# Two causal attentions of a decoder: later keys zeroed by a select on GpSimd after the exponential, in place of a mask product on TensorE before it

## The chip, the cores and the metric

The kernel runs on one core of one Trainium2 chip. The metric is the device time of one execution in microseconds (us), the median of several runs. Each engine works through its own queue of instructions in order and waits on semaphores that other engines raise: TensorE (PE in the profile, with its weight loads as PEld), VectorE (DVE), ScalarE (ACT), GpSimd (POOL) and SyncE (SP, which here issues DMAs).

## The reference, cut to what matters

The program is a decoder of twelve sub-layers on x of 16 x 256 tokens x 128. Several of them hold attentions with a softmax; the change touches two that are causal, both with 16 heads of width 8. One is the self-attention inside `L0_xattn`:

```python
att = jnp.einsum('bhqd,bhkd->bhqk', q, k) * scale
causal = jnp.tril(jnp.ones((T, T), bool))
att = jnp.where(causal[None, None], att, -jnp.inf)
y = jnp.einsum('bhqk,bhkd->bhqd', jax.nn.softmax(att, axis=-1), v)
...
y = y + jnp.einsum('bhqk,bhkd->bhqd', jax.nn.softmax(attc, axis=-1), vc)
```

The other is `_mha` inside `L2_ffn`, with rotary q and k:

```python
causal = jnp.tril(jnp.ones((s, s), dtype=bool))
scores = jnp.where(causal, scores, -jnp.inf)
attn = jax.nn.softmax(scores, axis=-1)
y = jnp.einsum('bhqk,bhkd->bhqd', attn, v)
```

## The kernel before, in words

Each attention is an object of class `SelfAttention`; `program` makes those two with mode "causal": s1 (the first attention below; it also carries the cross-attention, `cross=True`) and s8 (the second; `rope=True`). Work goes by **units**, one batch element each, 16 per attention, and by **slots**: every engine has a method `*_slot(e, g)` that is called with g = 0, 1, 2, ... and issues what this engine has to do in slot g. The order on each queue is thus fixed by those methods; nothing reorders it. A unit starts every 10 slots in s1 and every 8 in s8. In its slots 0 to 7 the maxima pass runs, one pair of heads (s and 8 + s) per slot; in its slots 12 to 19 (LE = 12) the exponentials pass runs on the same pairs. Since these overlap with the next unit's maxima, a usual slot holds both.

**Maxima pass.** `pe_max` (L1235) multiplies q by k for two heads into PSUM banks that three rotating tiles share, `pe_max_mask` (L1253) adds a large negative mask of later keys by a product of an identity (bf16) with a 128x128 mask for both diagonal blocks (256 columns), and `dve_max` (L1269) takes row maxima. At the unit's end L1278 joins two of them, `dve_neg_max` (L615, L617) negates and splits them, `pe_mbt` (L626) turns them, ScalarE copies them (L635), and SP writes them as extra rows of q, so that the second product of q and k comes out with the maximum already subtracted.

**Exponentials pass.** `pe_exp` (L1362) writes the scores with keys on the partitions and queries along the row, two heads in two of three banks: 256 columns for the first key block and 128 for the second, 384 in all; columns 0 to 127 and 256 to 383 are the diagonal blocks. `pe_exp_mask` (L1378) adds the mask to these two blocks by one product of 256 columns per head, and signals `st`. `act_exp` (L1322) takes the exponential into PT, which holds four pairs. Two slots later, in slots with odd s, `pe_pv` (L1417) multiplies two pairs of PT by the values, 16 products; the 9th column of the values is one and gives the sum of the exponentials. `act_tv`, `pe_tvt` (L659), `dve_norm` (L670, L676) and `pe_oot` (L699) finish a unit.

**Everything else in the slots.** Every two units `Tail` does the output product (L281), the residual (L295) and the norm. Its inverse root is seeded on VectorE by L418, L420, L422 and refined on GpSimd by `newton`, three rounds of the four lines L429, L431, L433, L435, each of which waits for the one before. In s8 the norm also takes L351, L352 on GpSimd and L365, L367, L377 on VectorE. q and k are split into three bf16 parts (ScalarE L571, L577; GpSimd `pool_rest` L582 and `pool_lo` L588) and stacked by DMA; in s8 VectorE L1089 and GpSimd L1096 (`pool_rope`) rotate them first. In s1 GpSimd also adds the cross part (L1462).

Of the kernel before, what the change touches and what calls it, by code (L numbers as in the profile page):

```python
# [8 lines left out]
ALU = mybir.AluOpType  # L9
# [891 lines left out]
def twice(mask):  # L901
    return mask.rearrange("p (o k) -> p o k", o=1).to_broadcast([128, 2, 128])


class SelfAttention(Heads):


    LE, MBT, CMBT, TV, GATE = 12, 9, 11, (5, 9, 11), 8

    def __init__(self, K, prev, W, mode, rope=False, reps=1, gate=False, cross=False, kind="ln", g=None, lead=0, ring=0, again=False):  # L910
# [8 lines left out]
        LE, L = self.LE, 10 if cross else 8  # L919
# [3 lines left out]
        start = [P + s for s, _, _ in rows]  # L923
# [14 lines left out]
        nu = len(units)  # L938
# [29 lines left out]
        self.st = K.ev("scores", 2 * nu * self.nx)  # L968
        self.exp = K.ev("exp", nu * self.nx if mode == "bias" else 2 * nu * self.nx)
        self.biased = K.ev("scores_biased", nu * self.nx if mode == "bias" else 0)  # L970
        self.pv = K.ev("pv", nu * self.np)
        self.tv = K.ev("tv", nu * self.nf)
        self.tvt = K.ev("tv_turned", nu * self.nf)
# [373 lines left out]
    def pe_exp(self, e, u, s):  # L1347
        K, mode = self.K, self.mode
        b, r = self.units[u]
        c, bb = b // 2, b % 2  # L1350
        x = self.nx * u + s
        plain = mode == "none"
        if s == 0:
            e.wait_ge(*self.shift.at(u))
        self.banks_free(e, x)
        lo = 128 if self.causal else 0
        rows = self.mrow + 2
        for kt in range(2):
            for i in self.heads(x):
                q1 = K.QS[self.set(c)][64 * i:64 * i + rows, s, 256 * bb + lo * kt:256 * bb + 256]  # L1360
                k1 = K.KS[self.set(c)][64 * i:64 * i + rows, s, 256 * bb + 128 * kt:256 * bb + 128 * kt + 128]
                k = e.matmul(self.st_bank(x, i)[:, 256 * kt:512 - lo if kt else 256], k1, q1, start=kt == 0,  # L1362
                             stop=plain and kt == 1)
                if plain and kt == 1:
                    k.then_inc(*self.st.inc())

    def pe_exp_mask(self, e, u, s):
        K, mode = self.K, self.mode
        if mode == "none":
            return  # L1370
        x = self.nx * u + s
        for i in self.heads(x):
            hh = 8 * i + s
            s_ = self.st_bank(x, i)
            if mode == "bias":
                k = e.matmul(s_[:, 256:384], K.idf[:, :], self.bias.KB[:, hh, 0:128], start=False, stop=True)
            elif mode == "causal":
                k = e.matmul(s_.rearrange("p (a k) -> p a k", a=2)[:, :, 0:128], K.idb[:, :], twice(K.mskK[:, :]), start=False,  # L1378
                             stop=True)
            elif mode == "add":  # L1380
                diag = s_.rearrange("p (a k) -> p a k", a=4)[:, 0:4:3, :]
                k = e.matmul(diag, K.idb[:, :], twice(self.mask[:, 256:384]), start=False, stop=True)  # L1382
            k.then_inc(*self.st.inc())

    def dve_bias(self, e, u, s):

        K = self.K
        x = self.nx * u + s
        lo = self.BANKS[x % 2][0]
        st = K.PS[:, lo:lo + 2, 0:256]  # L1390
        e.wait_ge(*self.scored(x))
        e.tensor_tensor(st, st, self.bias.KB[:, s:16:8, :], ALU.add).then_inc(*self.biased.inc())  # L1392

    def pt_free(self, x):

        if x < 4:
            return None
        u, s = divmod(x - 4, self.nx)
        return self.pv.at(self.np * u + (s // 2 if s < 8 else s - 4))

    def pe_pv(self, e, u, j):
        K = self.K
        c, bb = self.units[u][0] // 2, self.units[u][0] % 2
        f = self.nf * u + j // 2
        x = self.nx * u + 2 * j
        if j % 2 == 0 and f > 0:
            e.wait_ge(*self.tv.at(f - 1))
        if j == 0 and bb == 0 and self.units[u][1] == 0:
            e.wait_ge(*(self.vact if self.W["vb"] is None else self.vdve).at(c))
        e.wait_ge(*self.exp_done(x + 1))  # L1410
        g = j % 2
        for kt in range(2):
            for i in range(4):
                lo = 128 if kt == 1 and self.causal else 0
                o = 256 if kt == 1 else 0
                pt = K.PT[:, (x + i // 2) % 4, 0:2 * self.width].rearrange("p (a k) -> p a k", a=2)
                k = e.matmul(K.PS[32 * i:32 * i + 9, 6, 256 * g + lo:256 * g + 256],  # L1417
                             K.VA[self.set(c)][:, (2 * bb + kt) * 16 + 8 * (i % 2) + 2 * j + i // 2, :], pt[:, i % 2, o:o + 256 - lo],
                             start=kt == 0, stop=kt == 1)
        k.then_inc(*self.pv.inc())  # L1420
# [271 lines left out]

    def pool_slot(self, e, g):
        K, LE = self.K, self.LE
        u = self.at(g, self.OOS - 1)
        if u is not None and (self.gate or self.cross):
            self.pool_join(e, u)
        c = self.out_at.get(g + 3)
        if c is not None and self.W["ob"] is not None:
            self.tail.pool_bias(e, c)  # L1700
        for off in (1, 4, 6):
            c = self.out_at.get(g - off)
            if c is not None:
                self.tail.pool(e, c, off)
        if self.rope:
            for n, kind, key in self.splits_at.get(g + 1, []):
                self.pool_rope(e, n)
        for n, kind, key in self.splits_at.get(g - 1, []):
            if kind != "setup":
                self.pool_lo(e, n, self.source(n, kind, key))  # L1710
        for n, kind, key in self.splits_at.get(g, []):
            if kind != "setup":
                self.pool_rest(e, n, self.source(n, kind, key))
# [198 lines left out]
class CrossAttention(Heads):  # L1912
# [5 lines left out]
    LE, turns = 5, 5  # L1918
# [2640 lines left out]
```

## Time and profile before

| what | value |
|---|---|
| median of 3 runs | 4510.38 us (4504.48 to 4520.68) |
| the profiled execution, its own time | 4514.29 us |
| its span in the profile | 4512.5 us |
| mean granted TensorE clock | 0.855 of full speed |
| busy, share of span | PE 77%, DVE 62%, ACT 46%, POOL 26% |

How to read it: all times inside the profile are of one execution, counted from the start of its span. A busy share is an average over stages whose limits differ. Matmuls are pipelined and the ends of their rows are modelled, so their starts, and those of the weight loads, tell more than their lengths. "Idle before" at the end of a row is how long this engine had been idle, and "<-" what ended it; "issue" means that nothing the profile shows was waited for. Rows with xN merge N neighbours.

### The profile page before, as it was taken

To read this page: it belongs to the slowest core of one execution; us is meant where nothing else is said; L and a number is where in the kernel's file an instruction comes from. 1 tells how busy PE (TensorE), PEld (TensorE's weight loads), DVE (VectorE), ACT (ScalarE), POOL (GpSimd) and SP (SyncE) were. 2 spreads that over 40 slices of the span, in tenths; PEclk is the share of its full clock that TensorE was granted. 3 is DMA by queue.
4 is the path that set the end of the run, shared out by engine and by line. 5 is a ranking of instruction groups with operands and counts; after the bars stand their busy time and mean duration, and the time that the engine had idled before them with its cause. 6 is when DMAs were issued, how large, how long until landed. Compare 5 with 4: busy or idle time off the path is not lost. (4 is left out here: it accounts for less than half of the span.)

```text
span 4512.5 us, 86659 instructions
## 1 busy us (share of the span) xinstructions
PE 3476.0 (77%) x30682; PEld 2227.5 (49%) x30682; DVE 2808.6 (62%) x7618; ACT 2086.9 (46%) x4656; POOL 1181.7 (26%) x2276
## 2 busy tenths in 40 slices
PE   5877888886887668738989989756994558858992
PEld 1443554453555447713444444333552445648992
DVE  4884675365786665625777767457774376865563
ACT  2664665223343535414666666443562034425661
POOL 2322221021111234520111110124321242133565
PEclk9987998797998769957999999767996579979996
DMA  4323321023220322212121110132332050022332
GB/s 96 52 34 56 56 54 22 17 90 49 34 34 16 62 65 75 75 33 34 33 34 32 30 31 17 23 63 41 56 46 67 15 155 19 5 84 77 108 95 67
DMA packets 316471, 231.39 MB, mean 51 GB/s; under 512 B 45267, under 2 KB 300848, under 8 KB 315868
## 3 DMA queue, kind: packets, MB, share of 16 engines
q1 hardware_dynamic: 303116, 199.36, 22.1%
q0 software_dynamic: 12928, 26.50, 1.9%
q8 instruction: 248, 4.06, 0.4%
q14 instruction: 179, 1.47, 0.1%
HBM read 68.43 MB, written 55.53 MB: 27 GB/s over the span
## 5 line engine op out<-in xcount | busy, mean ns | idle before, releaser
L1322 ACT ACTIVATE PT<-ps 128x512 f32<-128x512 f32 (+1 forms) x1600 | 812.0, 559 | 519.7 <-PE ps L1382 274.4
L1272 DVE TENSOR_REDUCE M<-ps 128x2 f32<-128x512 f32 x1024 | 655.6, 684 | 289.4 <-PE ps L1256 262.0
L1235 PE MATMUL ps<-SKB 49*128 49x256 bf16 (+2 forms) x3584 | 434.2, 280 | 170.9 <-DMA SKB<-HH 74.0
L1269 DVE TENSOR_REDUCE M<-ps 128x3 f32<-128x384 f32 x768 | 390.5, 550 | 187.2 <-PE ps L1253 122.0
L1417 PE MATMUL ps<-PT,VA 128*9 128x256 f32 (+1 forms) x7168 | 451.4, 371 | 1.5 <-ACT PT L1322 1.0
L1362 PE MATMUL ps<-SKB 51*128 51x256 bf16 (+2 forms) x3584 | 366.1, 271 | 88.5 <-DMA SKB<-MT 70.5
L3675 ACT ACTIVATE SKB<-ps,SKB 128x128 f32<-128x128 f32 x1032 | 295.2, 370 | 254.8 <-PE ps L3595 253.5
L1235 PEld LDWEIGHTS ps<-SKB 48*128 48x128 bf16 (+1 forms) x3584 | 138.4, 95 | 475.2 <-issue 157.5
L3737 DVE COPY SKB<-SKB 128x1028 f32 (+1 forms) x258 | 187.3, 726 | 235.1 <-PE ps L3604 206.8
L582 POOL TENSOR_TENSOR FF<-FF,HH 128x512 f32<-128x512 f32 (+1 forms) x118 | 128.8, 1092 | 605.2 <-ACT HH L571 605.0
L3595 PE MATMUL ps<-SKB 128*128 128x128 f32 x2064 | 286.3, 284 | 0.0
L3604 PE MATMUL ps<-SKB 128*128 128x128 f32 x2064 | 282.2, 281 | 3.6 <-ACT SKB L3675 3.6
L3595 PEld LDWEIGHTS ps<-SKB 128*128 128x128 f32 x2064 | 263.0, 199 | 0.4 <-issue 0.3
L3604 PEld LDWEIGHTS ps<-SKB 128*128 128x128 f32 x2064 | 260.4, 198 | 4.5 <-ACT SKB L3675 4.5
L3512 POOL DMA_INDIRECT L_sorted_rows<-XT,GG x192 | 196.9, 1026 | 246.2 <-DVE SKB L3744 120.2
L1417 PEld LDWEIGHTS ps<-PT,VA 128*9 128x9 f32 x7168 | 155.2, 91 | 199.8 <-issue 95.2
L1362 PEld LDWEIGHTS ps<-SKB 50*128 50x128 bf16 (+1 forms) x3584 | 176.7, 98 | 149.8 <-DMA SKB<-MT 81.4
L429 POOL TENSOR_TENSOR NW<-NW 128x4 f32<-128x4 f32 x336 | 69.4, 206 | 656.6 <-DVE NW L422 628.5
L3570 POOL DMA_INDIRECT PT<-L_sorted_results,GG x192 | 196.4, 1023 | 131.0 <-issue 50.7
L659 PE MATMUL ps<-idf,TV 128*128 128x128 f32 x1088 | 177.8, 288 | 33.1 <-ACT TV L650 16.2
L1313 ACT ACTIVATE PT<-ps 128x768 f32<-128x768 f32 x128 | 103.8, 811 | 212.3 <-DVE ps L1392 212.3
L1052 PE MATMUL ps<-XT,WB 128*128 128x512 f32 x224 | 152.7, 769 | 49.4 <-DMA SKB<-in_c_one 29.2
(487 smaller groups left out, 6760.2 us busy)
## 6 DMA issues: line engine op xcount, KB each, us to landing
SKB<-HH SPq DMA_DIRECT2D x1224, 64.0 KB
SKB<-HH SPq DMA_DIRECT2D x576, 32.0 KB
PT<-L_sorted_rows SPq DMA_DIRECT2D x258, 64.0 KB
L_sorted_results<-SKB SPq DMA_DIRECT2D x258, 64.0 KB
SKB<-in_L3f_w SPq DMA_DIRECT2D x32, 256.0 KB, 3.3
L_sorted_rows<-TV SPq DMA_DIRECT2D x2, 4032.0 KB, 29.0
SKB<-scratch SPq DMA_DIRECT2D x2, 2048.0 KB, 10.6
SKB<-in_L1f_w SPq DMA_DIRECT2D x16, 256.0 KB, 3.2
```

Of the source, the lines that this page charges most:

```text
L1235: k = e.matmul(self.mx_bank(m + i)[:, o:o + n], K.QS[self.set(c)][64 * i:64 * i + rows, s, 256 * bb + 128 * qt:256 * bb + 128 * qt + 128], ...
L1269: k = e.tensor_reduce(K.M3[n % 2][:, hh, 0:3], mx[:, 0:384].rearrange("p (a k) -> p a k", a=3), axis=AX.X, op=ALU.max)
L1272: k = e.tensor_reduce(K.M3[n % 2][:, hh, 0:2], mx.rearrange("p (a k) -> p a k", a=2), axis=AX.X, op=ALU.max)
L1322: e.activation(K.PT[:, x % 4, n * i:n * i + n], self.st_bank(x, i)[:, 0:n], ACT.Exp, bias=0.0, scale=self.scale).then_inc(*self.exp.inc())
L1362: k = e.matmul(self.st_bank(x, i)[:, 256 * kt:512 - lo if kt else 256], k1, q1, start=kt == 0, stop=plain and kt == 1)
L1417: k = e.matmul(K.PS[32 * i:32 * i + 9, 6, 256 * g + lo:256 * g + 256], K.VA[self.set(c)][:, (2 * bb + kt) * 16 + 8 * (i % 2) + 2 * j + i / ...
L3512: e.indirect_dma_start(self.XS[h], bass.IndirectOffsetOnAxis(ap=D.IDX[:, col:col + 1], axis=0), K.XT[:, 128 * t:128 * t + 128], None).then ...
L3570: e.indirect_dma_start(self.YG[i % 8], None, self.YS[h], bass.IndirectOffsetOnAxis(ap=D.IDX[:, q:q + 1], axis=0)).then_inc(*self.gathered. ...
L3595: k = e.matmul(K.PS[:, 2 + m % 2, 128 * hc:128 * hc + 128], self.WT[m % 3][:, 128 * hc:128 * hc + 128], self.XC[m % 3], start=True, stop=True)
L3604: k = e.matmul(K.PS[:, 4 + m % 2, 0:128], self.HB[m % 3][:, hc, :], self.WT[m % 3][:, 512 + 128 * hc:640 + 128 * hc], start=hc == 0, stop= ...
L3675: k = e.activation(self.HB[n % 3][:, hc, :], K.PS[:, 2 + n % 2, 128 * hc:128 * hc + 128], self.func, bias=self.WT[n % 3][:, 1024 + hc:1025 ...
L3737: e.tensor_copy(self.WT[n % 3], self.table[:, bass.ds(at, TC)]).then_inc(*self.wt.inc())
```

## The change

In mode "causal", `pe_exp_mask` does nothing and `pe_exp` signals `st` itself. A new `pool_select` stands at the head of GpSimd's slot LE + 1 + s: it waits for the pair's second exponential and runs two `affine_select` instructions in place on PT, one per head, on both diagonal blocks (128 x 2 x 128 elements, f32); where query minus key is negative they write 0. The second signals `selected` (it uses the counter named scores_biased), and `pe_pv` waits for it instead of for the exponential. The mask of the maxima pass stays. The four-deep PT and all other orders stay. The exponential is now also taken of later keys' scores, and the result overwritten.

```diff
@@ SelfAttention.__init__
+        self.selects = mode == "causal"
+        self.selected = K.ev("scores_biased", 8 * nu * self.selects)
@@ pe_exp
-        plain = mode == "none"
+        plain = mode == "none" or self.selects
@@ pe_exp_mask
-        if mode == "none":
+        if mode == "none" or self.selects:
             return
...
-            elif mode == "causal":
-                k = e.matmul(s_.rearrange("p (a k) -> p a k", a=2)[:, :, 0:128], K.idb[:, :], twice(K.mskK[:, :]), start=False,
-                             stop=True)
+    def pool_select(self, e, u, s):
+
+        x = self.nx * u + s
+        e.wait_ge(*self.exp_done(x))
+        for i in range(2):
+            diag = self.K.PT[:, x % 4, 384 * i:384 * i + 384].rearrange("p (b k) -> p b k", b=3)[:, 0:3:2, :]
+            k = e.affine_select(diag, diag, [[0, 2], [1, 128]], ALU.is_ge, 0.0, base=0, channel_multiplier=-1)
+        k.then_inc(*self.selected.inc())
@@ pe_pv
-        e.wait_ge(*self.exp_done(x + 1))
+        e.wait_ge(*(self.selected.at(8 * u + 2 * j + 1) if self.selects else self.exp_done(x + 1)))
@@ pool_slot
+        hit = self.inside(g, LE + 1, 8)
+        if hit and self.selects:
+            self.pool_select(e, *hit)
```

TensorE's queue in s8, a slot that ends in the value products. Before (PT holds exponentials, ps is PSUM, SKB the stacked q and k):

```order
L1235 MATMUL ps<-SKB 128x128 [waits mx_free] x2
L1235 MATMUL ps<-SKB 128x256 x2
L1362 MATMUL ps<-SKB 128x256 [waits exp]
L1362 MATMUL ps<-SKB 128x256
L1362 MATMUL ps<-SKB 128x128 x2
L1253 MATMUL ps<-mskQ,idb 128x2x128 x2
L1378 MATMUL ps<-mskK,idb 128x2x128 x2
L1417 MATMUL ps<-PT,VA 9x256 [waits exp]
```

The same slot in the changed kernel (its lines stand 3 to 9 further down):

```order
L1238 MATMUL ps<-SKB 128x128 [waits mx_free] x2
L1238 MATMUL ps<-SKB 128x256 x2
L1365 MATMUL ps<-SKB 128x256 [waits exp]
L1365 MATMUL ps<-SKB 128x256
L1365 MATMUL ps<-SKB 128x128 x2
L1256 MATMUL ps<-mskQ,idb 128x2x128 x2
L1426 MATMUL ps<-PT,VA 9x256 [waits scores_biased,tv]
```

The two products of L1378 are gone, and the value products wait for a select.

GpSimd's queue in s8 around the Newton steps of a tail (NW, RSD: the root; FF, HH: a split). Before:

```order
L351 TENSOR_TENSOR X<-X,RR 128x512
L352 TENSOR_TENSOR RR<-RR 128x512
L1096 TENSOR_TENSOR FF<-FF,GG 128x512
L582 TENSOR_TENSOR FF<-FF,HH 128x512
L429 TENSOR_TENSOR NW<-NW 128x4
...
L435 TENSOR_TENSOR RSD<-NW 128x4
L588 TENSOR_TENSOR HH<-FF,HH 128x512
L1096 TENSOR_TENSOR FF<-FF,GG 128x512
```

And in the changed kernel, from the end of the selects of one stretch to the next:

```order
L351 TENSOR_TENSOR X<-X,RR 128x512
L352 TENSOR_TENSOR RR<-RR 128x512
L1099 TENSOR_TENSOR FF<-FF,GG 128x512
L1400 AFFINE_SELECT PT<-PT 128x2x128 x2
L582 TENSOR_TENSOR FF<-FF,HH 128x512
L1400 AFFINE_SELECT PT<-PT 128x2x128 x2
L429 TENSOR_TENSOR NW<-NW 128x4
...
L435 TENSOR_TENSOR RSD<-NW 128x4
L588 TENSOR_TENSOR HH<-FF,HH 128x512
L1400 AFFINE_SELECT PT<-PT 128x2x128 x12
```

One pair's selects (x2) now stand on either side of L582, and those of six further pairs (x12) behind L588; four tails of s8 look like this, in the last ones the split (L582, L588) is absent.

## Rows read from the trace of the kernel before

**Rows 1.** The page: busy time by engine, and the chain that ended last.

```profile
PE 3476.0 (77%) x30682; PEld 2227.5 (49%) x30682; DVE 2808.6 (62%) x7618; ACT 2086.9 (46%) x4656; POOL 1181.7 (26%) x2276
...
PE 5%; POOL 1%; issue 1%; DVE 1%; DMA 0%; DVEq 0%; ACT 0%; POOLq 0%
```

**Rows 2.** Windows over s1 and s8: length, busy per engine, PEclk, DMA share, GB/s.

```profile
423.00:752.00 329.00, 297.76 (x3378) 169.48 (x3374) 228.15 (x698) 206.56 (x463) 78.63 (x151) 0.95 0.26 50
3163.00:3413.00 250.00, 235.77 (x2815) 133.12 (x2814) 185.21 (x491) 156.62 (x350) 71.80 (x131) 1.00 0.30 48
```

**Rows 3.** The mask product, L1378: count, min/median/max ns; who waited for it.

```profile
L1378 PE MATMUL ps<-mskK,idb x512: 272/273/421, 423.5 to 3412.8; 128*128 128x256 bf16 x171
...
  ACT PT L1322: 154.6, 191
```

**Rows 4.** Waits: total us, times, longest; first in s8, then in s1.

```profile
PEld ps L1235 <- DVE M L1269: 23.7, 56, 1.5
...
PEld ps L1235 <- DVE M L1269: 18.5, 46, 0.8
```

**Rows 5.** Timeline, TensorE's weight loads, s8, two slots: start, us, engine, line.

```profile
3344.48 0.11 PEld L1253 LDWEIGHTS ps<-mskQ,idb 128*128 128x128 bf16 x2 [0.16 <-issue]
3344.61 0.21 PEld L1378 LDWEIGHTS ps<-mskK,idb 128*128 128x128 bf16 x2
3345.02 0.09 PEld L1235 LDWEIGHTS ps<-SKB 48*128 48x128 bf16 x1 [0.21 <-issue]
3345.41 0.11 PEld L1235 LDWEIGHTS ps<-SKB 48*128 48x128 bf16 x3 [0.30 <-DVE M L1269]
...
3346.39 0.55 PEld L1417 LDWEIGHTS ps<-PT,VA 128*9 128x9 f32 x16 [0.21 <-issue]
3347.16 0.11 PEld L1235 LDWEIGHTS ps<-SKB 48*128 48x128 bf16 x4 [0.22 <-issue]
```

**Rows 6.** Timeline, weight loads, s8 before its first exponentials (no L1378 yet).

```profile
3153.48 0.11 PEld L1253 LDWEIGHTS ps<-mskQ,idb 128*128 128x128 bf16 x2 [0.16 <-issue]
3153.81 0.09 PEld L1235 LDWEIGHTS ps<-SKB 48*128 48x128 bf16 x1 [0.21 <-DVE M L1269]
```

**Rows 7.** Groups of instructions on GpSimd, whole run: busy us, mean ns, idle before.

```profile
L582 POOL TENSOR_TENSOR FF<-FF,HH 128x256 f32<-128x256 f32 x16 | 10.8, 675 | 50.1 <-ACT HH L571 50.1
...
L4285 POOL MEMSET SKB<- 128x2048 f32 x1 | 1.8, 1805 | 0.0
...
L3517 POOL MEMSET TV<- 128x128 f32 x2 | 0.4, 205 | 6.3 <-ACT XT L393 6.3
```

**Rows 8.** Timeline, GpSimd, s8, around one root.

```profile
3313.55 1.28 POOL L1096 TENSOR_TENSOR FF<-FF,GG 128x512 f32<-128x512 f32 x1 [5.43 <-DVE GG L1089]
3315.75 1.16 POOL L582 TENSOR_TENSOR FF<-FF,HH 128x512 f32<-128x512 f32 x1 [0.92 <-ACT HH L571]
3317.01 0.20 POOL L429 TENSOR_TENSOR NW<-NW 128x4 f32<-128x4 f32 x1
...
3320.10 0.20 POOL L435 TENSOR_TENSOR RSD<-NW 128x4 f32<-128x4 f32 x1
3320.25 1.16 POOL L588 TENSOR_TENSOR HH<-FF,HH 128x512 bf16<-128x512 f32 x1
```

**Rows 9.** Timeline, the same stretch: two exponentials, and the value products' weight loads.

```profile
3311.74 0.87 ACT L1322 ACTIVATE PT<-ps 128x384 f32<-128x384 f32 x2 [1.93 <-PE ps L1378]
3313.65 0.87 ACT L1322 ACTIVATE PT<-ps 128x384 f32<-128x384 f32 x2 [1.04 <-PE ps L1378]
...
3318.42 0.55 PEld L1417 LDWEIGHTS ps<-PT,VA 128*9 128x9 f32 x16 [0.21 <-issue]
...
3321.91 0.55 PEld L1417 LDWEIGHTS ps<-PT,VA 128*9 128x9 f32 x16 [0.21 <-issue]
```

**Rows 10.** Timeline, the same stretch: a small VectorE operation and TensorE's wait behind it.

```profile
3315.77 1.16 DVE L422 TENSOR_SCALAR NW<-NW 128x4 int32<-128x4 int32 x1
...
3317.44 0.11 PEld L1235 LDWEIGHTS ps<-SKB 48*128 48x128 bf16 x3 [1.49 <-DVE M L1269]
```

## The prediction, made before the changed kernel ran

> **What bounds the kernel now.** I read the page first. TensorE is the busiest engine, and the chain that ended last covers only 8% of the span, the experts at the very end [rows 1]; it says nothing of the two causal attentions. So I went to the windows over them [rows 2]. TensorE is busy 298 of 329 us (91%) in s1 and 236 of 250 (94%) in s8, at a granted clock of 0.95 and 1.00; VectorE stands at 69% and 74%, ScalarE at 63%, GpSimd at 24% and 29%. A slot of s8 lasts 250 / 128 = 1.95 us, one of s1 some 2.2 (16 units of 10).
>
> The waits say where TensorE is not the limit: in 56 slots of s8 and 46 of s1 its next maxima product waits for VectorE's reduce to free a bank [rows 4]. The two slots of the timeline show both kinds [rows 5]. In the first, weight loads go L1378, one L1235, and then stop 0.30 us until a reduce is done: whatever is taken from TensorE there, it waits longer. In the second, the value products follow, and the next L1235 waits for issue alone. ScalarE waits for the mask product 191 times, 154.6 us [rows 3], but it has that time to spare.
>
> **What goes.** 2 x 8 x 16 x 2 = 512 mask products [rows 3], two in each of 256 slots. The rows price the two by difference: from L1253's load to the next L1235's first load is 0.33 us where no L1378 stands between [rows 6]. With it, the same stretch is 3345.02 - 3344.48 = 0.54 us [rows 5]. So a slot gives back 0.21 us, where TensorE is what the slot waits for. In s8 that is 128 - 56 = 72 slots. In s1 128 - 46 = 82, less some 17 (my count on the timeline) at the units' ends that wait for the cross-attention's maxima: 65. 137 x 0.21 = **29 us gained**. In the other slots I cost the removal at nothing: VectorE's reduce covers it, and its chain is not touched. The exponential also starts earlier, but its bank comes free in time already, so this gains nothing.
>
> **What comes.** 512 selects on GpSimd, two per slot. No row shows one. From below: a write-only fill takes 205 ns for 128 columns and 1805 for 2048, 0.83 ns a column, so 0.31 us for 256 [rows 7]. From above: a sum of two tensors, 256 columns, takes 0.675 us [rows 7]; and this form has two blocks with a gap, which might add to that. A select reads one tensor, so I take a little under the middle: 0.45 us, **0.9 us a pair**, with 0.31 and 0.7 as ends.
> The Trainium skill (GPSIMD Engine Reference, 3.1) puts its best loop without branches at 1.8 cycles an element, 769 ns for 512; an estimate from that for 256 elements is 0.38 us plus dispatch, 0.5 to 0.6. By it a pair is about 1.1 us, and the sum below would end near 4511 us instead of 4504. No row here decides between the two.
>
> Load on GpSimd: 29% of 1.95 us is 0.57 us a slot, with a pair 1.5 us. It fits, on average. What counts is the queue. A select stands behind whatever GpSimd has in its slot, and the value products of slots with odd s need the pair of two slots before. From the end of the exponential at 3313.65 + 0.87 to the products at 3318.42 that is 3.9 us [rows 9], elsewhere down to some 2.5. It does not do where a norm's root stands in the queue. I walk through it in s8 [rows 8, 9]:
> - L1096 ends at 3313.55 + 1.28 = 3314.83. The exponentials that begin at 3311.74 are long done, so their select runs from there to 3315.75.
> - L582 follows at its old time, to 3316.9. The pair of 3313.65 is selected by 3317.85; value products at 3318.42 need it, in time.
> - The root, 3.29 us from L429's start to RSD's end, now begins at 3317.9 and ends at 3321.2; L588 at 3322.4.
> - Two pairs are selected behind it, by 3324.2. The value products of 3321.91 need the second: **they are 2.3 us late.**
>
> TensorE is in order, so the next maxima and scores are late as well, and VectorE and ScalarE behind them. Four roots of s8 have a split beside them and cost 2.3 us each; three have none and cost 2.3 - 1.16 = 1.1; the eighth lies behind the last unit. That is 12.5, say **13 us lost in s8**. In s1 slots are longer and the root stands two slots further from the value products that need it; I allow 0.4 us for each of 8, **3 us**, an allowance that no row gives.
>
> **The port.** A small VectorE operation on SBUF (L422, otherwise 0.17) took 1.16 us while L582 ran, and TensorE then waited 1.49 us for the reduce behind it [rows 8, 10]. Each unit has some three clusters of such operations (L1278; L615 with L617; the tail's). GpSimd will be in a select 0.9 of every 1.95 us; half a select remains on average, 0.22 us. 32 units x 3 x 0.46 x 0.22 = 10 us on VectorE, of which I put two thirds, **7 us**, on the path.
>
> **Sum.** -29 + 13 + 3 + 7 = -6 us against the profiled execution's 4514.3: 4508. That execution was 3.9 us over the median, so as a median of runs 4510.4 - 6, about **4504 us**. A measurement of this kernel can tell about 0.3%, 13.5 us, from no change; my forecast lies inside that.
>
> **Rivals.**
> 1. *The selects are cheap and hidden.* At 0.31 us a select the pair is 0.6; each root then costs 4 x 0.3 = 1.2 us less (four pairs lie between L1096 and the late value products): 4 x 1.1 + 0 = 4 us in s8, nothing in s1, the port 4. Sum -21: 4489. If the slack is also larger than I see, the whole 29 stays: 4481. For it: a select reads one tensor. Against: selects are in the queue four deep around each root even then. Chance 0.28.
> 2. *The queue of GpSimd becomes the wait.* At 0.7 us a select the pair is 1.4, and four of them add 2.0 us to each root: 4 x 4.3 + 3 x 3.1 = 26 us in s8, 8 in s1, the port 12. Sum +17: **4527**. It decides against the change from a pair of about 1.05 us (0 gain) on. For it: the row for two tensors; and two blocks with a gap. Against: no second operand. Chance 0.20.
> 3. *GpSimd becomes the bound of s8.* If a select costs 1.0 us, pair and other work are 2.0 + 0.57 = 2.6 us a slot against 1.95: 128 x 0.6 = 80 us more in s8, about 20 in s1: 4600. Only an operation slower than every elementwise row of its size would do that. Chance 0.07.
> 4. *The clock.* s8 runs at 1.00 and s1 at 0.95 [rows 2]; if waits for selects let the granted clock fall in part of the stretches, 5% of 579 us is 29 us more, 4533. Such waits do occur in s1 today and it keeps 0.95. Chance 0.05.
> That the change doesn't do what it says I put at nothing: the products are gone from the queue and only their mask is.
>
> **How the numbers follow.** The forecast has 0.40, with its own range 4495 to 4514. Rival 1 and the forecast's lower edge give faster by over 0.3% (under 4497): 0.28 + 0.06 = 0.34. The rest of the forecast, and a part (0.04) of rival 2 near its point, is within 0.3%: 0.38. Slower: 0.16 + 0.07 + 0.05 = 0.28. The range takes in rival 1 down to the whole gain and rivals 2 and 4 with some margin, and leaves rival 3 out: 4480 to 4545.
>
> **What would show it.** L1378's place in the timeline empty and L1253 to L1235 at 0.33 us; AFFINE_SELECT rows of 0.45 us, 512 of them; waits of L1417 for PT from GpSimd, few, over 1 us, behind L588 after a root; L1278 and L615 more often at several times 0.17. s8 some 10 us or less shorter with s1 5 to 10 shorter. I am wrong if L1417 never waits for a select (rival 1), or waits in most slots (rival 3), if the select's mean is outside 0.31 to 0.7, or if TensorE's waits for VectorE grow by the whole 29 us.

## The result, and the profile after

The changed kernel takes 4526.8 us against 4509.4 for the kernel before (medians of 19 runs each on one chip); the ratio is 1.0035, interval 1.0027 to 1.0043. It is **slower by some 16 us**, where I had forecast 6 us less. The profiled execution took 4524.1 us, span 4522.3.

The page after, busy time by engine, and two groups of its part 5:

```profile
PE 3448.9 (76%) x30170; PEld 2181.4 (48%) x30170; DVE 2825.6 (62%) x7618; ACT 2085.8 (46%) x4656; POOL 1368.4 (30%) x2788
...
L1426 PE MATMUL ps<-PT,VA 128*9 128x256 f32 (+1 forms) x7168 | 462.8, 379 | 13.0 <-POOL PT L1400 11.7
...
L1400 POOL TENSOR_SCALAR_AFFINE_SELECT PT<-PT 128x256 f32<-128x256 f32 x512 | 192.9, 407 | 108.6 <-ACT PT L1325 107.5
```

Against [rows 1], TensorE has 512 matmuls fewer and is busy only 27 us less. The select takes 407 ns. (Lines have moved: L1235 is now L1238, L1253 L1256, L1269 L1272, L1278 L1281, L1417 L1426, L1089 L1092; the select is L1400.)

To see where the time lies I cut s8 at TensorE's output product (L281 of `ot`), which comes once in two units: seven pairs of units. Windows, kernel before: us; busy of PE, PEld, DVE, ACT, POOL; PEclk (the granted clock). The whole stretch, then pairs 1, 3, 5 and 7:

```profile
3202.97:3418.02 215.05, 199.17 (x2409) 112.84 (x2406) 155.88 (x427) 133.62 (x298) 61.03 (x122) 1.00 0.29 45
3202.97:3236.14 33.17, 31.93 (x375) 18.09 (x373) 26.44 (x70) 20.67 (x46) 11.74 (x20) 1.00 0.36 58
...
3269.31:3303.49 34.18, 31.77 (x375) 18.15 (x372) 26.50 (x70) 20.75 (x46) 11.80 (x20) 1.00 0.37 57
...
3337.67:3366.69 29.02, 27.27 (x359) 16.09 (x356) 22.03 (x66) 18.30 (x41) 4.66 (x14) 1.00 0.28 44
...
3396.16:3418.02 21.86, 17.38 (x213) 8.53 (x212) 5.46 (x23) 14.17 (x32) 4.66 (x14) 1.00 0.04 14
```

The same windows of the changed kernel:

```profile
3196.41:3430.51 234.10, 202.09 (x2194) 102.17 (x2192) 167.70 (x426) 133.52 (x298) 141.17 (x341) 0.88 0.25 41
3196.41:3234.39 37.98, 32.24 (x342) 16.46 (x341) 28.53 (x68) 20.90 (x47) 23.48 (x54) 0.91 0.27 51
...
3272.21:3309.88 37.67, 33.34 (x342) 16.87 (x341) 28.47 (x68) 20.90 (x47) 23.46 (x54) 0.86 0.31 52
...
3347.49:3375.56 28.07, 24.86 (x326) 13.14 (x325) 23.60 (x64) 17.98 (x42) 17.27 (x49) 1.00 0.29 45
...
3403.68:3430.51 26.83, 20.33 (x190) 9.24 (x190) 6.99 (x26) 13.92 (x32) 13.47 (x38) 0.63 0.04 11
```

Pairs 5 and 6, which have no split, gained 0.9 and 1.4 us. Pairs 1 to 4, which have splits, lost 3.4 to 4.8 us each, and their granted clock fell from 1.00 to between 0.86 and 0.91. Pair 7, the last, has no split and no maxima pass of a next unit any more; it lost the most, 5.0 us, at a clock of 0.63. With 215 matmuls fewer, TensorE is busy *longer* (202.1 against 199.2 us), and idle twice as long (234.1 - 202.1 = 32.0 against 15.9). Two things were lost, then: TensorE waits more, and it works at half clock in part of the stretch.

In s1 the first and last value products start 341.9 us apart (428.4 to 770.3), before 340.7 (429.0 to 769.7): its length held, though its clock fell too, from 0.96 to 0.91. The windows of [rows 2], after:

```profile
423.00:752.00 329.00, 285.97 (x3125) 150.07 (x3128) 231.04 (x696) 204.73 (x463) 163.86 (x385) 0.91 0.27 49
...
3163.00:3413.00 250.00, 218.40 (x2443) 111.14 (x2444) 189.91 (x472) 147.34 (x330) 155.69 (x359) 0.92 0.27 44
```

TensorE's waits in s8, changed kernel (total us, times, longest):

```profile
PE ps L1238 <- DVE M L1272: 13.0, 20, 1.8
PE ps L1426 <- POOL PT L1400: 10.7, 14, 1.6
```

The kernel before, in its s8:

```profile
PE ps L1235 <- DVE M L1269: 6.8, 21, 1.4
```

Both kinds of wait that the prediction named are there, and a place that it did not look at. Timeline, changed kernel, behind a split without a root:

```profile
3306.11 1.16 POOL L582 TENSOR_TENSOR FF<-FF,HH 128x512 f32<-128x512 f32 x1 [1.05 <-ACT HH L571]
3307.22 0.77 POOL L1400 TENSOR_SCALAR_AFFINE_SELECT PT<-PT 128x256 f32<-128x256 f32 x2
...
3308.14 0.84 PE L1426 MATMUL ps<-PT,VA 128*9 128x256 f32 x16 [1.00 <-POOL PT L1400]
```

The pair of selects stands behind L582, which itself waits for ScalarE's L571 at the end of the slot. Seven of the 14 waits for selects in s8 are this one, 1.00 us each. The forecast's place, behind a root:

```profile
3323.89 0.34 PE L1238 MATMUL ps<-SKB 48*128 48x128 bf16 x3 [1.75 <-DVE M L1272]
...
3326.15 0.50 PE L1238 MATMUL ps<-SKB 48*128 48x128 bf16 x4
...
3326.91 1.15 POOL L588 TENSOR_TENSOR HH<-FF,HH 128x512 bf16<-128x512 f32 x1
...
3328.01 2.92 POOL L1400 TENSOR_SCALAR_AFFINE_SELECT PT<-PT 128x256 f32<-128x256 f32 x8
...
3329.55 1.47 PE L1426 MATMUL ps<-PT,VA 128*9 128x256 f32 x16 [0.24 <-POOL PT L1400]
```

Here the wait is short, 0.24 us (1.59 at the first root), because TensorE came late itself: it had waited for VectorE 1.75 us at 3323.89, and in the rows from 3326.15 on it runs at the half clock (1.2 GHz): four L1238 take 0.50 instead of 0.34 us, sixteen L1426 1.47 instead of 0.84. The last such row of this place starts at 3334.19 (four L659, 1.06 instead of 0.66 us). The 1.75 us stand behind VectorE's seed: L420, otherwise 0.17 us, took 1.15 while L582 ran, and L422 0.32, as the next select began.

### The profile page after: what moved, and what is told of

It is laid out like the page before. It is cut to its first block and busy times, and to the rows that moved or that the text cites. A ratio compares the mean times of both kernels' runs of the same rounds, so it can differ in the third digit from the quotient of the medians.

```text
span 4522.3 us, 86148 instructions
## 1 busy us (share of the span) xinstructions
PE 3448.9 (76%) x30170; PEld 2181.4 (48%) x30170; DVE 2825.6 (62%) x7618; ACT 2085.8 (46%) x4656; POOL 1368.4 (30%) x2788
## 5 line engine op out<-in xcount | busy, mean ns | idle before, releaser
L1238 PE MATMUL ps<-SKB 49*128 49x256 bf16 (+2 forms) x3584 | 441.0, 282 | 183.7 <-DMA SKB<-HH 74.6
L1272 DVE TENSOR_REDUCE M<-ps 128x3 f32<-128x384 f32 x768 | 390.5, 550 | 195.8 <-PE ps L1256 131.4
L1426 PE MATMUL ps<-PT,VA 128*9 128x256 f32 (+1 forms) x7168 | 462.8, 379 | 13.0 <-POOL PT L1400 11.7
L1238 PEld LDWEIGHTS ps<-SKB 48*128 48x128 bf16 (+1 forms) x3584 | 140.5, 96 | 494.5 <-issue 151.2
L582 POOL TENSOR_TENSOR FF<-FF,HH 128x512 f32<-128x512 f32 (+1 forms) x118 | 128.6, 1090 | 550.5 <-ACT HH L571 550.2
L1426 PEld LDWEIGHTS ps<-PT,VA 128*9 128x9 f32 x7168 | 157.5, 92 | 219.8 <-issue 112.9
L1400 POOL TENSOR_SCALAR_AFFINE_SELECT PT<-PT 128x256 f32<-128x256 f32 x512 | 192.9, 407 | 108.6 <-ACT PT L1325 107.5
L659 PE MATMUL ps<-idf,TV 128*128 128x128 f32 x1088 | 180.5, 291 | 37.7 <-ACT TV L650 16.1
```

The lines of the kernel that those rows point to most:

```text
L1238: k = e.matmul(self.mx_bank(m + i)[:, o:o + n], K.QS[self.set(c)][64 * i:64 * i + rows, s, 256 * bb + 128 * qt:256 * bb + 128 * qt + 128], ...
L1272: k = e.tensor_reduce(K.M3[n % 2][:, hh, 0:3], mx[:, 0:384].rearrange("p (a k) -> p a k", a=3), axis=AX.X, op=ALU.max)
L1400: k = e.affine_select(diag, diag, [[0, 2], [1, 128]], ALU.is_ge, 0.0, base=0, channel_multiplier=-1)
```

## The experiments

All kernels below are measured against the kernel before on the same chip, several times, so ratios are compared and not microseconds. "Pairs" is the stretch of seven pairs as above; idle is its length less TensorE's busy time. Both come from one profiled execution of each kernel. Where s8 is unchanged they repeat well (before, s1_only, s1_again and s1_head: 214.7 to 215.2 us), but not every profiled execution is a typical one: that of s8_even was the slowest of its 12 (4585 us, median 4565), those of s8_head, s8_rounds and s8_rest were the fastest of theirs.

| kernel | ratio, interval | pairs us | PE busy | idle | PEclk |
|---|---|---|---|---|---|
| before | 1 | 215.1 | 199.2 | 15.9 | 1.00 |
| the change | 1.0035 [1.0027, 1.0043] | 234.1 | 202.1 | 32.0 | 0.88 |
| s8_only | 1.0055 [1.0039, 1.0071] | 232.8 | 201.7 | 31.2 | 0.89 |
| s1_only / s1_again | 0.9988 [0.9975, 1.0002] / 0.9986 [0.9975, 0.9997] | 215.1 / 214.7 | | | 1.00 |
| s1_head | 1.0005 [0.9991, 1.0018] | 215.2 | | | 1.00 |
| s8_no_mask | 0.9994 [0.9982, 1.0005] | 209.8 | 186.1 | 23.7 | 0.98 |
| s8_beside | 1.0015 [0.9999, 1.0030] | 222.3 | 191.0 | 31.3 | 0.95 |
| s8_both | 1.0054 [1.0034, 1.0073] | 238.3 | 208.4 | 29.9 | 0.96 |
| s8_head | 1.0086 [1.0068, 1.0103] | 240.8 | 203.5 | 37.3 | 0.88 |
| s8_rounds | 1.0079 [1.0056, 1.0101] | 240.6 | 201.8 | 38.8 | 0.89 |
| s8_short | 1.0018 [1.0006, 1.0031] | 219.8 | 190.8 | 29.1 | 0.94 |
| s8_rest | 0.9986 [0.9976, 0.9996] | 212.7 | 199.0 | 13.7 | 1.00 |
| s8_no_mask_rest | 0.9963 [0.9951, 0.9976] | 202.8 | 182.7 | 20.2 | 0.99 |
| s8_seed | 0.9991 [0.9975, 1.0007] | 211.5 | 199.3 | 12.3 | 1.00 |
| s1_seed | 0.9980 [0.9965, 0.9994] | 211.6 | | | 1.00 |
| all_seed | 1.0105 [1.0085, 1.0125] | 262.9 | 207.8 | 55.1 | 0.86 |
| s8_even | 1.0002 [0.9988, 1.0015] | 218.3 | 195.4 | 22.9 | 0.99 |

### Which attention

```diff
-        self.selects = mode == "causal"
+        self.selects = mode == "causal" and not cross     # s8_only; "and cross": s1_only
```

(with the mask product put back for the other one).

> The change in s8 alone; s1 keeps its mask products. All theories: the loss sits in s8, since the trace of the changed kernel has s1 the same length within 2 us and s8 18 us longer: about 4509 + 17 = 4526, ratio 1.003 to 1.004. If s1 carries half of it: 4518.

> The change in s1 alone. If the loss sits in s8: 4509 to 4511, no difference beyond 0.1%. If s1 carries half of the loss: 4518.

The loss is s8's: 1.0055. s1 alone lies under 1 in two measurements, 0.9988 and 0.9986, of which the second excludes no change: some 6 us gained. In their profiled executions the first and last value products of s1 start 335.2 and 332.6 us apart, against 340.7 before, at a clock of 0.94 and 0.95; in the whole change, at 0.91, this gain was not there. The product of the two ratios, 1.004, fits the whole change within the intervals.

### The removal alone, the selects alone

s8_no_mask drops products and selects. s8_beside has no products either, and selects that write a buffer nobody reads, so that TensorE does not wait for them. s8_both keeps the products and adds selects and waits:

```diff
 # s8_beside, in pool_select
-            diag = self.K.PT[:, x % 4, 384 * i:384 * i + 384]...
+            o = 1024 * (x % 4) + 384 * i
+            diag = self.K.BIG[:, o:o + 384]...
 # s8_both, in pe_exp
-        plain = mode == "none" or self.selects
+        plain = mode == "none"
```

> s8 without its 256 mask products and without selects (later keys on the diagonal blocks are left in). Queue theory (the loss comes from value products that wait behind GpSimd's queue, and the clock falls after those waits): the removal alone gains, 72 slots of 0.21 us = 15 us, 4494, and the granted clock of s8 stays at 1.00. Clock theory (less TensorE work by itself lowers the granted clock): the clock of s8 falls below 0.95 here too, and the time is 4505 to 4515.

> s8 without its mask products; the same 256 selects run on an unused part of SBUF at the same place of GpSimd's queue, and no engine waits for them (later keys are left in). Queue theory: within 5 us of s8_no_mask, about 4497, clock 1.00. Port theory (the small VectorE operations that a select holds up carry the loss): most of the loss is here already, 4515 to 4525.

> s8 with the selects and their waits, and with the mask products kept: TensorE does the old work and the selects are awaited. Queue theory: the wait for selects costs the same or a little less than in the change in s8 alone (there 1.0055 of before), and the products' removal gave next to nothing, so 1.004 to 1.006. Clock theory (the freed TensorE time is what lowers the clock): the clock of s8 is back near 0.97 and the ratio is 1.001 to 1.003, below the change itself, though it does more work.

Three readings. First, the removal gives 5 us of the stretch, where 15 were forecast for all of s8 and 12.7 for the 215 of 256 products in the stretch. Pairs without a split gain 1.5 to 2 us, pair 1 gains 0.6, pairs 2 to 4 nothing or less. The timeline of s8_no_mask, in pair 1, shows one reason:

```profile
3242.14 1.15 POOL L582 TENSOR_TENSOR FF<-FF,HH 128x512 f32<-128x512 f32 x1 [0.74 <-ACT HH L571]
3242.28 1.04 DVE L422 TENSOR_SCALAR NW<-NW 128x4 int32<-128x4 int32 x1
...
3243.83 0.11 PEld L1237 LDWEIGHTS ps<-SKB 48*128 48x128 bf16 x3 [1.52 <-DVE M L1271]
```

The root's seed (L422) runs into L582 and takes 1.04 us instead of 0.17, until L582 is done; TensorE waits 1.52 us for the reduce behind it. Before, pairs 1 and 2 (33.2 us) missed this and pairs 3 and 4 (34.2) had it [rows 10]; with faster slots all four have it (L422 1.04, 1.04 and 1.00 us, in pair 4 L420 1.17). The other reason is the clock, 1.00 in pair 1 and 0.95 in pairs 2 to 4. TensorE in the same place of pair 1 and of pair 2, s8_no_mask:

```profile
3243.84 0.34 PE L1237 MATMUL ps<-SKB 48*128 48x128 bf16 x3 [1.39 <-DVE M L1271]
...
3244.59 0.84 PE L1428 MATMUL ps<-PT,VA 128*9 128x256 f32 x16
...
3276.42 0.33 PE L1237 MATMUL ps<-SKB 48*128 48x128 bf16 x3 [1.39 <-DVE M L1271]
...
3277.46 1.47 PE L1428 MATMUL ps<-PT,VA 128*9 128x256 f32 x16
```

The wait is the same, and so is the pair's idle time (2.8 us). Behind it pair 1 goes on at full speed and takes 32.6 us; pair 2 goes on at the half clock and takes 34.0. Nothing waits for GpSimd's selects here, for there are none.

Second, selects that TensorE doesn't wait for cost 12.5 us of the stretch (209.8 to 222.3): 7.6 more idle, 4.9 more busy for the same matmuls. VectorE's groups in it, s8_beside:

```profile
L377 DVE TENSOR_SCALAR RR<-RR,RSD 128x128 f32<-128x128 f32 x28 | 9.9, 413 | 2.8 <-POOL RSD L435 2.8
L615 DVE TENSOR_SCALAR MB<-M 128x16 bf16<-128x16 f32 x26 | 9.1, 351 | 0.1
...
L420 DVE TENSOR_SCALAR NW<-NW 128x4 int32<-128x4 int32 x7 | 5.1, 730 | 0.2
...
L365 DVE TENSOR_REDUCE BS<-RR 128x4 f32<-128x512 f32 x7 | 4.8, 680 | 3.4 <-POOL RR L352 3.4
```

and in s8_no_mask, the same kernel without selects:

```profile
L377 DVE TENSOR_SCALAR RR<-RR,RSD 128x128 f32<-128x128 f32 x28 | 6.1, 280 | 0.0
...
L615 DVE TENSOR_SCALAR MB<-M 128x16 bf16<-128x16 f32 x26 | 4.5, 172 | 0.1
...
L420 DVE TENSOR_SCALAR NW<-NW 128x4 int32<-128x4 int32 x7 | 2.2, 313 | 0.2
```

L377, L615 and L420 are small operations from SBUF to SBUF, and they grow where GpSimd runs; VectorE as a whole is busy 14.4 us longer with the same 427 instructions. The reduce, which reads PSUM, does not grow: L1272 has a mean of 550 ns here and 551 in the kernel before. The Trainium skill (SBUF — State Buffer, "Who interferes with whom") says that VectorE and GpSimd share one pair of SBUF ports, held for a whole instruction, which a `tensor_scalar` from SBUF can contend for and a reduce never does. L422 ending with L582 agrees.

But s8_beside does not show the port alone. The selects also stand in GpSimd's queue, and VectorE waits for what comes late behind them: 3.4 us for L352 and 2.8 us for the root (L435), one time each, both in pair 7, which grew by 4.4 of the 12.5 us. No run parts these two causes. The clock is in it as well. Pairs 2 and 3 of s8_beside:

```profile
3264.66:3299.26 34.60, 30.14 (x340) 15.11 (x340) 28.97 (x69) 20.69 (x47) 23.39 (x53) 1.00 0.32 55
3299.26:3336.23 36.97, 33.66 (x340) 16.71 (x341) 28.90 (x69) 20.69 (x47) 23.40 (x53) 0.86 0.34 53
```

Third, waiting for the selects adds another 10.5 us (222.3 to 232.8), and of that **nothing is idle time**: idle is 31.3 and 31.2, busy 191.0 and 201.7. The matmuls, the same but for two, take 10.7 us longer, at a clock of 0.89 instead of 0.95. This is not one odd execution: over the whole kernel the mean granted clock was 0.845 to 0.849 in all 6 runs of s8_only, 0.847 to 0.855 in the 12 of s8_beside, and 0.850 to 0.857 in the 29 of the kernel before beside them. In s8_both the clock stays higher, 0.96, and TensorE does 215 matmuls more. That the added work is what kept the clock up is not shown. The ratio is that of s8_only, but the intervals would hide the 5 us that the removal is worth, and the stretch is 5.4 us longer than in s8_only. By the stretches, then, the removal of the products is still worth about what it was alone, too little to pay for the selects.

### The place of the select

s8_head and s1_head put the select at the head of its own slot, ahead of L582; s8_rounds also spreads the root's three Newton rounds over three slots:

```diff
-        hit = self.inside(g, LE + 1, 8)
+        hit = self.inside(g, LE, 8)
         if hit and self.selects:
```

> The change in s8 alone, with the select at the head of its own slot of GpSimd's queue (LE + s), before the root, the rotation and the splits, not one slot later behind them. Queue theory: the waits of the value products for selects halve (8.5 to 11 us before), a pair of units with splits goes from 37.6 us to about 35.5, ratio 1.002 to 1.003. Clock or port theory: no change, 1.0055.

> As the one before, and the three Newton rounds of a root stand in three slots with a select between them, not in one block of 3.3 us; VectorE's and TensorE's steps that use the root move one slot down. Queue theory: waits for selects nearly vanish (under 3 us), a pair of units 34.5 us, ratio 0.999 to 1.002, down to what selects cost that nobody waits for (1.0015 was measured). If it stays at 1.003 or more, waiting is not what the loss is made of.

> The change in s1 alone (0.9988 of before), with the select at the head of its own slot. Queue theory: the few waits left in s1 go, 0.997 to 0.9985. Port theory: as before, 0.9988.

The two in s8 came out at 1.0086 and 1.0079, slower than s8_only by 8 us of the stretch each (by the ratios alone the intervals touch). Waits in s8_head, over its pairs:

```profile
PE ps L1238 <- DVE M L1272: 20.4, 19, 3.0
...
DVE BS L365 <- POOL RR L352: 11.5, 7, 5.4
...
PE ps L1429 <- POOL PT L1403: 3.3, 3, 1.4
```

TensorE's waits for selects fell from 6.6 us (s8_only, same stretch) to 3.3, as wanted. But GpSimd is in order: the work behind the select, L351 and L352, comes later, VectorE's L365 waits for it, and the reduces queued behind L365 are late. The wait changed engines and grew. s8_rounds is the plainer answer: its waits for selects are down to 2.0 us in 2 times, under the 3 us expected, and it is as slow, with the same 11.5 us of L365 behind L352. By what I had written beforehand, waiting for selects is then not what the loss is made of. In s1 the same move gave 1.0005 where 0.9988 stood, which the intervals do not part.

### Short selects, and a short L582

s8_short keeps selects and waits but covers 8 of 128 keys. s8_rest and s8_no_mask_rest shorten L582 in s8 to 8 of 512 columns, the first under the kernel before, the second under s8_no_mask:

```diff
 # s8_short
-            k = e.affine_select(diag, diag, [[0, 2], [1, 128]], ...)
+            n = 128 if self.cross else 8
+            k = e.affine_select(diag[:, :, 0:n], diag[:, :, 0:n], [[0, 2], [1, n]], ...)
 # s8_rest, s8_no_mask_rest
-                self.pool_rest(e, n, self.source(n, kind, key))
+                self.pool_rest(e, n, self.source(n, kind, key), 8 if ... else None)   # columns
```

> The change in s8 alone, but each select covers 8 of the 128 keys of its two diagonal blocks, so it is short (the other later keys stay in): the wait of TensorE on GpSimd's queue is kept, the work of the selects nearly gone. This splits what the selects cost in s8 (4590.84 us against 4564.81 without them, 26 us on that chip, 23 by the pairs of units) into queue and work. Theory A (GpSimd's instructions are what hurts: they hold VectorE's small operations up and make the selects come late): most of the loss goes, ratio 0.9995 to 1.002, pairs of units in s8 sum to 211 to 218 us, VectorE's L422 as without the change. Theory B (the place in GpSimd's in-order queue behind L582 and the twelve instructions of the root is what hurts, however short the select): ratio 1.004 to 1.006, pairs 226 to 233, waits of the value products on GpSimd 5 us or more.

> The kernel before, with GpSimd's subtraction L582 in s8 on 8 of 512 columns (the rest of the split's remainder is left out): 32 instructions of 1.15 us become short. It is the mate of the next kernel. If GpSimd's L582 holds VectorE's L422 up in the third and fourth pair of units (34.2 us each beside 33.2 of the first and second), L422 falls from 1.16 to 0.17 us there, those pairs fall to about 33.2, and the stage gains 1 to 3 us: ratio 0.999 to 1.000. If the pairs differ for another reason, nothing moves.

> s8 without mask products and without selects (the later keys of the diagonal blocks stay in), and with L582 on 8 of 512 columns as in its mate. With L582 whole, leaving the 256 products out gave only 5 us of the stage instead of the 15 that 72 slots of 0.21 us promise. Theory A (the gain is given back in the collision of L422 with L582): against its mate this one gains 10 to 15 us, pairs of units sum to 198 to 204 us, ratio 0.9965 to 0.998. Theory B (the slots of s8 are paced by VectorE or ScalarE, and the products lie in waits anyway): against its mate again 3 to 6 us, pairs 207 to 210, ratio 0.9985 to 0.9995.

> The change in s1 alone once more, for a closer interval: the only version below the kernel before so far (0.9988, interval 0.9975 to 1.0002). Theory A (the selects of s1 are free and its 65 slots gain a little): 0.998 to 0.9995. Theory B (nothing: the pairs of units in s8 and the stage span of s1 did not move in the trace): 0.9995 to 1.0005.

A short select still takes 206 ns. Even so, of the 0.0061 between s8_no_mask and s8_only (28 us) it takes away 0.0037 (17 us), and 0.0024 (11 us) stays; in the stretch 13.0 us go and 10.0 stay. The two amounts by the ratios are uncertain by some 8 us each, so which part is larger is not shown. How it was saved is a surprise. TensorE's waits for selects over the pairs, s8_only and s8_short:

```profile
PE ps L1429 <- POOL PT L1403: 6.6, 9, 1.5
```

```profile
PE ps L1430 <- POOL PT L1404: 6.2, 8, 1.7
```

They are the same, as theory B had it. Of the 13.0 us 10.9 are busy time: the clock is 0.94 and not 0.89, with 1.00 in pairs 2 and 3 (33.9 us each) and 0.86 and 0.91 in pairs 1 and 4 (36.5 and 36.4). Theory A has the ratio; its stretch (211 to 218) is just missed, and L422 is held more than without selects (0.66 us on average, 0.54 in s8_no_mask). Neither theory holds alone.

The pair with the short L582 settles where the gain of the removal went. Windows of s8_rest, the whole and pair 3:

```profile
3218.09:3430.80 212.71, 199.02 (x2409) 112.98 (x2406) 149.75 (x426) 133.62 (x298) 53.32 (x122) 1.00 0.29 45
...
3284.34:3317.57 33.23, 31.78 (x375) 18.16 (x373) 24.95 (x69) 20.71 (x46) 9.86 (x20) 1.00 0.36 58
```

and of s8_no_mask_rest:

```profile
3222.60:3425.43 202.83, 182.68 (x2194) 94.67 (x2193) 150.38 (x426) 131.57 (x298) 53.52 (x122) 0.99 0.29 47
...
3285.71:3317.34 31.63, 29.60 (x342) 15.19 (x341) 25.11 (x68) 20.49 (x47) 9.91 (x20) 1.00 0.40 62
```

Pairs 3 and 4 fall from 34.2 to 33.2 us with the short L582, as said. Taking the products out now gains 9.9 us of the stretch, 1.6 in each of pairs 1 to 4, and of the whole time 0.9986 - 0.9963, some 10.5 us, where with the whole L582 it gained 0.0006, some 3. The intervals of these ratios would allow the same gain in both; the stretches, which repeat within 0.5 us, do not. That is the lower end of theory A (10 to 15), and its pairs (198 to 204) hold the 202.8.

### The seed at another place; half of the selects

s8_seed, s1_seed and all_seed put L365 to L422 two slots earlier in VectorE's order, under the kernel before, under s1_only and under the whole change. s8_even has the select in even slots and the mask product in odd ones, so that every select has a slot more before it is needed:

```diff
 # the seed
-        elif off == 5 and self.kind != "ln":
+        elif off == (3 if self.kind == "keep" else 5) and self.kind != "ln":
             self.dve_mean_square(e, c)
 # s8_even, in pe_pv
-        e.wait_ge(*(self.selected.at(8 * u + 2 * j + 1) if self.selects else self.exp_done(x + 1)))
+        e.wait_ge(*self.exp_done(x + 1))
+        if self.selects:
+            e.wait_ge(*self.selected.at(4 * u + j))
```

> The kernel before, with the sum of squares and the seed of the root of s8 (L365, L367, L418, L420, L422) put two slots earlier in VectorE's order, into the slot in whose gap VectorE waits for L1052. Theory A (GpSimd's L582 holds L422 up at its old place): L422 stays at 0.17 us in all pairs, the third and fourth pair fall from 34.2 to 33.2 or less, the stage gains 2 to 5 us: ratio 0.9985 to 0.9998. Theory B (the earlier place costs what it saves, since L1089 comes later): 0.9998 to 1.001.

> The change in s1 alone (0.9986 and 0.9988 in two measurements) with the seed of s8 two slots earlier as in its mate. If the two are independent the ratios multiply: with 0.9987 for s1 and 0.9985 to 0.9998 for the seed, 0.997 to 0.9985. A candidate for the fastest correct order.

> The whole change with the seed of s8 two slots earlier. Theory A (it is only the seed's small operations whose delay reaches TensorE): the hold is taken away and the ratio falls from 1.0035 to 1.000 or less. Theory B (with selects in every slot GpSimd is busy at any place the seed could have, and TensorE waits for selects too): 1.002 to 1.005, small operations of VectorE still held in some pairs, TensorE's waits for POOL PT still 8 us or more.

> In s8 the select for the even slots alone, the mask product for the odd ones: a value product takes the exponentials of an even and an odd slot, so that the select has a whole slot more before it is asked for. Half of the selects (64 pairs of 0.77 us less) and half of the removal. Theory A (the wait behind GpSimd's queue is the larger part): waits of TensorE for POOL near 0, ratio 0.999 to 1.001. Theory B (the selects' hold on VectorE is the larger part, half of it stays): 1.001 to 1.003, pairs 217 to 224.

s8_seed, the whole stretch and pair 3:

```profile
3224.48:3436.01 211.53, 199.28 (x2409) 112.00 (x2407) 155.31 (x427) 132.87 (x298) 60.86 (x122) 1.00 0.29 46
...
3290.55:3323.49 32.94, 31.99 (x374) 17.94 (x372) 26.34 (x70) 20.52 (x46) 11.74 (x20) 1.00 0.35 59
```

The collision is gone (L422 0.17 us in every record; another operation, L617, is held more, 314 ns on average against 181) and the stretch 3.5 us shorter, with all work done. The ratio, 0.9991, can't tell that from nothing by itself. With the change in s1 alone it is 0.9980 [0.9965, 0.9994], faster than both kernels: the product of the two (0.9978) within its interval.

Under the whole change the same move costs most of all, 1.0105. Waits of all_seed in its pairs:

```profile
DVE BS L365 <- POOL RR L352: 18.9, 7, 3.4
PE ps L1426 <- POOL PT L1400: 18.7, 14, 2.4
...
PE ps L1055 <- DVE FF L1092: 13.0, 4, 3.3
```

With selects in the queue L352 is no longer done two slots early, VectorE stands still on it, and everything in order behind it does too. My Theory B had the sign, not the size.

s8_even loses nothing, 1.0002; waits for selects fall to 0.9 us in 3 times, idle to 22.9, the clock is back at 0.99. The ratio is that of Theory A, the pairs (218.3, from the slowest of its runs) that of B. The wait is gone, as A said; that half of the removal now pays for half of the selects' hold fits, and is not shown.

## Why the prediction was wrong, point by point

**The step that failed** is the one that has no term in the sum: the clock, put at nothing there and at 0.05 as rival 4. The stretch of seven pairs splits like this. The 2194 matmuls that the change leaves are busy 182.7 us in s8_no_mask_rest, at a clock of 0.99, and 202.1 us in the change, at 0.88. So 16.5 us of work are gone (199.2 to 182.7) and 16.1 us of idle time have come (15.9 to 32.0). These two cancel, much as the sum had it for s8 (15 gained; 13 and a part of the port's 7 lost). What is left is 19.4 us of busy time at the lower clock, and the stretch is 19.1 us longer. Not all of that busy time is length, since TensorE waits less where it works slower: pair 3 of s8_beside has 3.5 us more busy time than pair 2 and is 2.4 us longer. By that share my estimate for the clock is 13 to 19 us of the stretch. Rival 4 with its 4533 came closer to the 4526.8 than the forecast did. The terms themselves:

- **The price of the select** was sized well: 0.407 us against my 0.45, a pair 0.77 against 0.9. My estimate from the Trainium skill (GPSIMD Engine Reference, 3.1), 0.5 to 0.6, was further off: the measurement decides. By my own figures this price lies between the forecast and rival 1, the gaining side: the sign was not lost here.
- **The term of -29 was too large in s8.** It said 72 slots of 0.21 us, 15 us, of which 12.7 belong to the stretch. s8_no_mask shows 5.2 us there, s8_no_mask_rest 9.9. One thing I left out is that faster slots move the seed into L582, a collision that stood in [rows 8, 10] and that I had priced only for the added selects. The other is that slots paced by TensorE become slots paced by VectorE once they are shorter: TensorE's weight loads wait for the reduce 45 times in the stretch before, 63 times in s8_no_mask and 66 in s8_no_mask_rest. In s1 the sum was right: 14 less 3 and its part of the port is some 7 us, and s1 alone gained some 6.
- **The term of +13** had the mechanism and not the places. TensorE waits for selects 10.7 us in s8's 14 waits. Seven of them, 7.0 us, are behind L582 in splits without a root, which I had not walked through; the root places have 2.7 us at four splits and under 1 at the others, where 9.2 and 3.3 were forecast, since TensorE was late there already. And what the awaited selects cost (s8_beside to s8_only, 10.5 us) was no idle time at all, but the clock.
- **The port, +7**, was too small. I had 10 us of hold on VectorE for all 32 units; s8_beside has 14.4 for the 14 units of the stretch, in the places I named and in more: L615 and L617 together 7.8 us, L377 3.8, the root's chain (L418, L420, L422) 1.4. How much of it reaches TensorE is not known: the 12.5 us that unwaited selects cost hold late work of GpSimd's queue and the clock too.
- **Rival 4, the clock, at 0.05.** I tied it to waits for selects. It fell without them too: to 0.98 over the stretch of s8_no_mask and 0.95 in s8_beside, where TensorE waits for VectorE. Between s8_beside and s8_only it is the whole difference, 10.7 us of busy time. My reason against it, that s1 has such waits and keeps 0.95, was a reading of another stage, and s1 fell to 0.91 itself, where TensorE waits for selects only 0.6 us, in 2 times.
- The median after, 4526.8, is that of rival 2 (4527), but its price, 0.7 us a select, was not the cause. The range held the time; the sign was wrong.

What stays open: the clock was never moved by itself. That the lower clock follows from the added waits is read from rows (full speed before the wait of 1.75 us, half some way behind it) and not shown by a run that changes the clock alone. The length of a wait does not decide it: 1.49 us leave the clock at 1.00 before, and in s8_no_mask the same 1.52 us leave it in pair 1 and are followed by the half clock in pair 2; the waits of 1.00 us behind the splits without a root have full speed on both sides. Nor does idle time in sum, which is equal in s8_beside and s8_only. The removal of the products can't be the whole answer either, since they are gone in pairs 1 and 2 of s8_no_mask alike. What made the 5.0 us of pair 7 was not tested.

## What to carry to other kernels

Work moved from the fullest engine to one at 29% isn't free: read the in-order queue it joins, and the engine whose small operations it holds up, slot by slot, to the end of every slot and not only around the one long item. A gain of 0.2 us a slot is real only if the shorter slot isn't then paced by another engine and doesn't bring two other instructions together; test the removal alone, with nothing in its place, before paying for a replacement. And price a wait of TensorE with the half-clock stretch that may follow it, not by its length.

## What the hardware showed that I had not expected

A select of 16 elements a partition takes 206 ns, one of 256 elements 407: a straight line through the two, which is an estimate, puts 0.19 us of the price on the instruction itself, about half at this size. A VectorE operation of 0.17 us held up by GpSimd takes up to 1.17 us, and one chain can pay twice: in the change L420 takes 1.15 us beside L582 and L422 behind it 0.32 beside a select, in each of the four roots with a split. TensorE with 215 fewer matmuls was busy longer, 202.1 against 199.2 us; the same matmuls took 182.7 at a clock of 0.99. And the same wait of TensorE in the same place of the same kernel was followed by full speed once and by the half clock the next time.
